# Moving the token statistics and the token normalisation of an attention kernel to other slots, two batches ahead

## The reference, cut to what matters

```python
h = jnp.maximum(_layernorm(x, axis=-1), 0.0)          # eps 1e-5
q, k, v = (split_heads(h @ W.T) for W in (Wq, Wk, Wv))
a = jnp.einsum('bhnd,bhmd->bhnm', q, k) * 512 ** -0.5 + (adj + adj)[:, None]
row_nonzero = jnp.any(a != 0, axis=-1, keepdims=True)
p = softmax(jnp.where(row_nonzero, a, -jnp.inf))      # NaN rows become 0
o = jnp.einsum('bhnm,bhmd->bhnd', p, v)
return x + merge_heads(o) @ Wo.T
```

## Time and profile before

| | before |
|---|---|
| median of 3 runs | 1273.17 us (1273.1 to 1274.94) |
| profiled execution | 1273.81 us, its span 1272.0 us |
| TensorE busy, matmuls | 1241.6 us (98%) |
| TensorE busy, weight loads | 1107.2 us (87%) |
| VectorE busy | 1112.8 us (87%) |
| ScalarE busy | 1050.6 us (83%) |
| GpSimd busy | 886.1 us (70%) |

### The profile page before, as it was taken

The page is one execution under the profiler, slowest core; times in us unless marked ns, Lnnn a source line. Parts: engine busy times, 40 slices in busy tenths (PEclk is TensorE's granted clock), DMA queues, the critical chain, the costliest instruction groups (busy, mean ns, idle before and its releaser), DMA issues. The chain is left out here.

```text
span 1272.0 us, 43970 instructions
## 1 busy us (share of the span) xinstructions
PE 1241.6 (98%) x13104; PEld 1107.2 (87%) x13104; DVE 1112.8 (87%) x4009; ACT 1050.6 (83%) x2427; POOL 886.1 (70%) x1268
## 2 busy tenths in 40 slices
PE   6899999999999999999999999999999999999997
PEld 5788898888888888988888988888888889888896
DVE  6788888989888888888888888898888988888987
ACT  5788888888888888888888888888888888888886
POOL 4767677776676776677776777766767766777765
PEclk9999999999999999999999999999999999999999
DMA  7345454464454454554554544644544545545533
GB/s 239 89 122 133 115 148 120 113 154 119 120 142 120 126 149 112 135 124 124 140 132 114 150 118 114 156 117 122 139 121 128 148 111 136 124 122 142 132 96 88
DMA packets 90772, 163.88 MB, mean 129 GB/s; under 512 B 14976, under 2 KB 23168, under 8 KB 90752
## 3 DMA queue, kind: packets, MB, share of 16 engines
q1 hardware_dynamic: 90752, 163.64, 49.5%
HBM read 46.14 MB, written 16.78 MB: 49 GB/s over the span
## 5 line engine op out<-in xcount | busy, mean ns | idle before, releaser
L984 POOL TENSOR_TENSOR fold<-minus 128x512 f32<-128x512 f32 x256 | 326.8, 1277 | 293.4 <-DVE bounds L794 293.4
L616 ACT ACTIVATE probs<-minus,bounds 128x256 f32<-128x256 f32 x1024 | 459.5, 499 | 23.4 <-DVE bounds L794 23.4
L803 DVE TENSOR_TENSOR pT_lo<-pT_ps,pT_hi 128x512 f16<-128x512 f32 x512 | 351.8, 687 | 64.2 <-ACT pT_hi L627 61.0
L794 DVE CUSTOM_DVE_ANT_0 minus<-s_ps,adj_now 128x256 f32<-128x256 f32 x1024 | 389.2, 418 | 8.0 <-ACT probs L616 4.8
L627 ACT ACTIVATE pT_hi<-pT_ps 128x512 f16<-128x512 f32 x512 | 304.9, 596 | 110.3 <-PE pT_ps L404 108.7
L404 PE MATMUL pT_ps<-ident,probs 128*128 128x128 f32 x2048 | 307.5, 273 | 1.7 <-ACT probs L616 1.6
L329 PE MATMUL job_ps<-hT_hi,w_hi 128*128 128x256 f16 x1024 | 280.2, 274 | 2.4 <-DVE hT_lo L758 2.4
L329 PE MATMUL job_ps<-hT_hi,w_lo 128*128 128x256 f16 x1024 | 278.9, 272 | 0.0
L329 PE MATMUL job_ps<-hT_lo,w_hi 128*128 128x256 f16 x1024 | 278.8, 272 | 0.0
L404 PEld LDWEIGHTS pT_ps<-ident,probs 128*128 128x128 f32 x2048 | 242.0, 141 | 19.0 <-ACT probs L616 2.5
L393 PE MATMUL s_ps<-qk_stack 96*128 96x256 f32 x1024 | 247.2, 323 | 1.2 <-DVE w_lo L744 1.2
(11 more groups left out here) (85 smaller groups left out, 2247.7 us busy)
## 6 DMA issues: line engine op xcount, KB each, us to landing
qk_stack<-qk_parts SPq DMA_DIRECT2D x768, 128.0 KB, 2.3
x_in<-x SPq DMA_DIRECT2D x32, 512.0 KB, 3.4
x_res<-x SPq DMA_DIRECT2D x32, 512.0 KB, 3.7
out<-y SPq DMA_DIRECT2D x64, 256.0 KB, 2.1
adj_in<-adj SPq DMA_DIRECT2D x32, 256.0 KB, 3.6
w_in<-wq SPq DMA_DIRECT2D x2, 512.0 KB, 5.8
w_in<-wk SPq DMA_DIRECT2D x2, 512.0 KB, 7.5
w_in<-wv SPq DMA_DIRECT2D x2, 512.0 KB, 9.5
```

The source lines that it names most:

```text
L616: end = nc.scalar.activation(probs[hh % 2][:, t, :], minus[hh // 2 % 2][:, hh % 2, t, :], ACT.Exp, bias=bounds[:, hh // 2 % 4, 2 * (hh % 2 ...
L794: end = nc.vector.tensor_tensor_reduce(out=minus[pair % 2][:, hh % 2, t, :], in0=s_ps[SCORE_BANK[hh]][:, t * N:(t + 1) * N], in1=adj_now[: ...
L803: nc.vector.tensor_tensor(pT_lo[hh % 4][:, :, :], pT_ps[hh % 2][:, :].rearrange("p (m n) -> p m n", m=NT), pT_hi[hh % 4][:, :, :], ALU.sub ...
L984: nc.gpsimd.tensor_tensor(f1[:, :, :], src[:, :, 0:N // 2], src[:, :, N // 2:N], ALU.add).then_inc(folded1, 1)
```

## The change

The tokens of batch b + 2, and not b + 1, are handled in body b. On VectorE `moments_of` is split: `tokens_stats` does the first tile's statistic at the end of slot 8, and at the end of slot 10 the second tile's; then `moments_of` waits and aggregates. On GpSimd `normalise(b + 2)` stands at slot 10. Both move out of slots 0 and 1. The loops of these two engines are one body shorter, and body 30 is written out; bodies 0 to 29 handle tokens, 30 and 31 none. On SyncE `load_tokens(b + 2)` stands first in a body, ahead of adj's load and `stack(1, b)`.

```diff
@@ sync
             def body(b, first, last):
+                if not (last or isinstance(b, int) and b + 2 == B):
+                    load_tokens(b + 2)
                 if not last:
                     sp.wait_ge(adj_copied, b + 1)
                     settled(sp, "sp")
                     sp.dma_start(adj_in[:, :, :], adj_d[b + 1]).then_inc(adj_loaded, 16)
                 stack(1, b, first)
-                if not (last or isinstance(b, int) and b + 2 == B):
-                    load_tokens(b + 2)
                 if not first:
                     store(b - 1, 0)
@@ vector
-            def moments_of(b):
+            def tokens_stats(b, tiles):
                 dve.wait_ge(x_loaded, (b + 1) * 16)
-                for t in range(NT):
+                for t in tiles:
                     end = nc.vector.bn_stats(stats[:, t, :], x_in[:, t, :])
                 end.then_inc(stats_done, 1)
-                dve.wait_ge(stats_done, b + 1)
+
+            def moments_of(b, steps):
+                dve.wait_ge(stats_done, steps)
                 settled(dve, "dve")
                 for t in range(NT):
                     end = nc.vector.bn_aggr(mean_var[:, t, :], stats[:, t, :])
...
-                    if not (first or last) and hh == 0:
-                        moments_of(b + 1)
+                    if not (nearly or last):
+                        if hh == 8:
+                            tokens_stats(b + 2, range(0, 1))
+                        if hh == 10:
+                            tokens_stats(b + 2, range(1, NT))
+                            moments_of(b + 2, 2 * (b + 2))
...
-            with dve.Fori(1, B - 1) as b:
-                body(b, False, False)
-            body(B - 1, False, True)
+            with dve.Fori(1, B - 2) as b:
+                body(b, False, False, False)
+            body(B - 2, False, True, False)
+            body(B - 1, False, False, True)
@@ gpsimd
-                    if not (first or last) and hh == 1:
-                        normalise(b + 1, False)
+                    if not (nearly or last) and hh == 10:
+                        normalise(b + 2, False)
...
-            with pool.Fori(1, B - 1) as b:
-                body(b, False, False)
-            body(B - 1, False, True)
+            with pool.Fori(1, B - 2) as b:
+                body(b, False, False, False)
+            body(B - 2, False, True, False)
+            body(B - 1, False, False, True)
```

More of the change, by code:

```diff
@@ L826, in factors @@
                                                o_sums[:, :, FREE], ALU.not_equal, ALU.mult).then_inc(factor_ready, 1)
-            moments_of(0)
+            tokens_stats(0, range(NT))
+            moments_of(0, 1)
             weight_extent(WQ, 0)
@@ L852, in _, with body @@
             shift(0, 1, True)
-            moments_of(1)
+            tokens_stats(1, range(NT))
+            moments_of(1, 2)
             take("qk", 2, 0)
-            def body(b, first, last):
+            def body(b, first, nearly, last):
                 for hh in range(HEADS):
@@ L871, in body @@
                     low_probs(b, hh, first and hh < 2)
-                    if not (first or last) and hh == 0:
-                        moments_of(b + 1)
-            body(0, True, False)
-            with dve.Fori(1, B - 1) as b:
-                body(b, False, False)
-            body(B - 1, False, True)
+                    if not (nearly or last):
[4 more added lines that the diff above has]
+                            moments_of(b + 2, 2 * (b + 2))
+            body(0, True, False, False)
+            with dve.Fori(1, B - 2) as b:
+                body(b, False, False, False)
+            body(B - 2, False, True, False)
+            body(B - 1, False, False, True)
             def last_low(k):
```

## The result

| | before | changed kernel |
|---|---|---|
| median | 1273.13 us (4 runs, 1273.04 to 1274.94) | 1261.61 us (4 runs, 1261.37 to 1263.86) |
| ratio | | 0.9908, 95% interval 0.9895 to 0.9921 |
| profiled execution, span | 1273.81, 1272.0 us | 1261.63, 1259.9 us |

0.9% faster, 1.6 us above the forecast of 1260.

What follows compares the result with a forecast made beforehand. TensorE's own stream plus waits repeating with the loop was taken to bound the kernel. Gain 0.83 less cost 0.37, times 30, is 13.8 us: 1273.8 to 1260.0; own range 1255 to 1269, 8-in-10 range 1247 to 1269.

Steps and rivals of the forecast that it cites:

- The gain of 0.83 a body: TensorE, first transposes to first output-projection product: without VectorE's 1.71 us of statistics, 10.91 us instead of 11.74; at worst 0.76.
- the 0.07: Slot 4's token transposes, absent from body 31: at worst 0.07 of their 0.35 us doesn't fit into a wait.
- The cost of 0.37 a body: Slot 12: TensorE waits 0.37 us for low half 11, late through the moved statistics; bounds 0.17 and 0.6.
- The copy of y1: ScalarE's copy, 0.85 us late behind slot 12, still done by 570.69 when TensorE's v0 wants it at 570.92.
- The sum: Whole run: 30 x (0.83 - 0.37) = 13.8 us off 1273.8, giving 1260.0.
- The range's lower end: Fastest time of the forecast's own range, 1255 us, from a loss of 0.17 with the full gain of 0.83.
- GpSimd: Normalisation of 3.1 us moved to slot 10: nobody waits for GpSimd; the copy of pair 6 has 1.2 us left.
- the 0.83 us need it: Slots 1 to 4: the gain requires moving GpSimd's normalisation, since otherwise h is too late for its earlier transposes.
- SyncE: Token load moved ahead of adj's load and 12 stack transfers: costs nothing, and lets store y0 go earlier.
- No new wait: Rival, 20%: TensorE loses nothing in slot 12; time 1248.9 us.
- the wait only moves: Rival, 9%: TensorE picks up ScalarE's lateness of 0.85 us between slots 12 and 15; time 1274.4 us.
- A loss of 1.27: Slower rival, 11%: no cover in slots 10 to 15, shift(13)'s lateness of 1.27 us reaches TensorE whole; 1287.0 us.

Runs made afterwards that it cites:

- e1: Changed kernel without the statistics and aggregations of batches 2 to 31; the normalisation waits for the loaded tokens instead: 1251.48 us, 0.9831 of the kernel before.
- e3: Changed kernel with the first statistic in slot 6, the second in slot 8, aggregations in slot 10: 1250.43 us, 0.9817 of the kernel before.
- e2: Changed kernel with both statistics and the aggregations at the end of slot 10, none in slot 8: 1276.16 us, 1.0019 of the kernel before.
- e7: Changed kernel with the first statistic in slot 6, second statistic and aggregations in slot 10: 1259.02 us, 0.987 of the kernel before.
- e4: Changed kernel with GpSimd's normalisation (batch b + 1) back in slot 1 and the token load behind the stack transfers: 1261.8 us, 0.9904 of the kernel before.
- e5: Changed kernel with only the token load put back behind the stack transfers: 1261.97 us, 0.9893 of the kernel before.
- e6: e3 with the token load put back behind the stack transfers: 1275.64 us, 1.0007 of the kernel before.

## Why the prediction was right, step by step

- **The gain of 0.83 a body** was 0.76: 38.64 to 37.88 (body 30 of the changed kernel, e1, e3), and 11.74 to 10.98 from T0 to y0. It is the lower end that I gave. The term that was off is the 0.07: the four token transposes that body 31 lacks do not fit wholly into the wait of y0 (0.35 us of transposes into 0.29 of wait). Taking two bodies of one trace that differ by the work in question gave the term to 0.07 us.
- **The cost of 0.37 a body** was 0.33 (38.20 less e1's 37.87), in the place and by the chain that I followed; shift(13) and low half 11 came within 0.03 us. e2 (0.8 lost when nothing is absorbed ahead), e7 (0.2) and e3 (none) vary the absorbed part and the time follows. Behind slot 12 nothing was lost, as worked out: slots 13 to 15 take what they took before. The copy of y1, worked out as 0.85 late, was 0.8 late (603.46 - 33.43 = 570.03, against 569.24 in the earlier trace rows) and ended 0.28 us before v0 started, at 604.32.
- **The sum.** 0.83 - 0.37 = 0.46 against 0.43 measured, 0.9 us over thirty bodies. Here luck helped: both terms were too large, by 0.07 and 0.04, and the errors cancel in part; the gain's alone would have been 2.1 us over thirty bodies. The rest of the difference between the 13.8 us forecast and the 12.1 us of the spans lies outside the loop. Body 0 pays 0.72 instead of 0.37: it has no y jobs in slots 12 and 13, so its TensorE follows VectorE there, and its o job waits 0.30 us for the qk take (row below). I had counted body 0 as a body like the others. The 0.44 before T0 lies inside the scatter of the prologue, whose instructions are the same: in the other executions T0 of body 0 comes between 35.7 and 39.5 us. The range's lower end was also added up 1 us too high: 1273.8 - 30 x (0.83 - 0.17) is 1254.0, not 1255.

```profile
66.05 0.66 PE L369 MATMUL job_ps<-ident,o 128*128 128x128 f32 x4 [0.30 <-DVE qk_parts L770]
```

- **GpSimd.** That its move costs nothing is right (e4, with the same time). The statement that "the 0.83 us need it" is wrong: e4 has the whole gain with the normalisation in slot 1. I left h where it was and moved only TensorE; but GpSimd's fold ahead of it waits for VectorE's shift, and this came earlier by the very statistics that were taken away. The moments themselves were never what it waited for: in the earlier trace rows they are done by 577.53, and the normalisation starts at 581.40, behind GpSimd's fold and division. In e4 it starts 5.8 us after T0, in the kernel before 7.5.
- **SyncE.** The load's place costs and gives nothing (e5). That it lets the store of y0 go earlier is wrong: the store is issued 17.4 us after T0 in the changed kernel and in e5 alike. The place pays only for a statistic in slot 6, and there it is worth twice the change: e6's median is 25.2 us above e3's, and from T0 of body 0 to T0 of body 31 their profiled executions differ by 22.1.
- **The rivals.** No new wait: its price, 1248.9, was nearly that of e3, and it failed on this change for the reason given, more work inserted than absorbed. That the wait only moves has its price in e2, but not by its mechanism: e2 loses in slot 12 and nothing in slots 13 to 15, where the rival put it. A loss of 1.27 was not seen in any version. The Trainium skill's rule of the most-contended engine (Perfetto Trace Analysis, Identifying the Most-Contended Engine) didn't decide here: with VectorE's sum at 1112.8 and 1109.2 us and the weight loads' at 1107.2 and 1108.9, the time fell by 0.9%, and in e3, with 1108.1 and 1108.0, by 1.8%.

## What to carry to other kernels

When the busiest engine is at 98% and its helper at 87%, look for gaps that repeat with the loop, and for a body of the same trace that lacks the suspected work: the two bodies give the gain before anything is built. Work taken out of the helper's queue isn't free where it goes. Insert it in portions that the helper's idle times can absorb before the next portion comes (in e3 the first of 0.60 us is absorbed whole by two idle times of 0.33 and 0.34, and 0.13 of the second is left), and count what stands behind the last idle time before the next product that the busy engine wants. When one wait is taken away, everything that was late through it comes earlier too, transfers and other engines' work included: date those anew before calling anything late.

## What the runs showed of the hardware that I had not expected

- Two aggregations (128x6 to 128x2) hold VectorE's queue for 0.15 us when their statistics are long done (e3) and for 0.29, and a wait of 0.15 before, when they follow a statistic.
- Of two loads of 512 KB issued 1.1 us apart the second takes longer: tokens land 4.9 us after issue in the changed kernel, right behind the load of x_res, and 3.4 in their old place behind the stack transfers. The load of x_res takes 3.7 us in both. In body 0, where no x_res goes ahead, the token load takes 3.3 us in the changed kernel too.
- The prologue of the same instructions took 35.7 to 39.5 us from one execution to the next, up to 0.3% of the run. The nine profiled executions fall into two groups. In four (both kernels, e1, e6) it took 36.1 us or less; in the other five 37.9 or more, and in these alone TensorE's first scores wait 2.6 to 2.9 us for the first stack transfers. In e7:

```profile
28.47 0.77 PE L393 MATMUL s_ps<-qk_stack 96*128 96x256 f32 x2 [2.82 <-DMA qk_stack<-qk_parts]
```

- The times of the loop's bodies were steady to 0.03 us wherever no transfer was waited for, so they tell small changes apart where the total doesn't.
